# Gated attention with a ternary feed-forward block: decay factors turned by DMA as 16-bit halves instead of by TensorE, and a new order of the work

## The chip, the cores and the metric

The kernel runs on one core of a Trainium2 chip. The metric is the device time of one execution in microseconds; the median of several executions is compared.

## The reference

For x of shape 8 x 1024 x 256 the block adds three terms. What this case touches is `Gc`, one decay factor per token and head, which multiplies the state sum on its way out.

```python
def _L0_attn_ref(x, Wq, Wk, Wv, Wo, gw, sw):        # H = 16 heads of d = 16
    Q, K, V = ((x @ W.T).reshape(B, L, H, d) for W in (Wq, Wk, Wv))
    KV = jnp.einsum('blhd,blhe->blhde', K, V)
    g = jnp.clip(jax.nn.sigmoid(x.reshape(B, L, H, d) @ gw.T), 1e-06, None)
    log_c = jnp.clip(jnp.cumsum(jnp.log(g), axis=1), -30.0, 30.0)
    Gc = (jnp.exp(log_c) + 1e-06)[..., None]
    R = jax.nn.silu(K @ sw.T)[..., None]
    S = jnp.cumsum(KV * R / Gc, axis=1) * Gc
    return jnp.einsum('blhd,blhde->blhe', Q, S).reshape(B, L, D) @ Wo.T

def _L0_ffn_ref(x, fast_b, w_fc, w_proj, u, v, gate):  # hidden 1024, rank 16
    h = _bitlinear(x, w_fc) + gate * (x @ v.T @ fast_b.T @ u.T)
    r = jnp.maximum(h, 0.0)
    return _bitlinear(r * r, w_proj)

xn = _layernorm(x)
return x + _L0_attn_ref(xn, ...) + _L0_ffn_ref(xn, ...)
```

## The kernel before

The tokens are cut into 32 units (b, u) of 256 tokens, each of two chunks c of 128: eight batches, four units each. All engines are programmed by hand, each with its own instruction stream: a `prologue` for the first units, a `slot` that is repeated for the units n = 3 to 29, and an `epilogue`. Within a stream the order is written out, one call per step; a step begins with its waits on semaphores and nothing behind it on that engine can pass it. `slot(b, u)` names its steps by the unit they work on: `prev`, (b, u), `nxt`, `after`, or `unit_after(b, u, k)` for the k-th unit ahead.

The steps for one unit are these. VectorE and ScalarE normalise the tokens (`stats_of`, `rstd_guess`, `refine_rstd`), GpSimd writes them (`normalise`, `xt_low`) and SyncE turns them with a transposing DMA (`turn_tokens`, two 16-bit parts, 1024 columns). TensorE makes queries (`queries_t`, bank front_b), keys (`keys`, bank front_a), values and gates (`values_gates`, front_b) and the cumulated logarithms (`cumulate`, front_a). ScalarE and VectorE take them out of the banks in a high and a low 16-bit part (`queries_high`, `queries_low` and so on), and SyncE spreads them over the lanes with DMAs (`stack_queries` eight, `stack_keys` four). Then per chunk: four `scores` products groups, each masked by VectorE (`mask`), `values` (32 column-tiled products), `state_update` and `carried` on TensorE, `carry_state` and `chunk_out` on VectorE. The feed-forward part is four quarters of `hidden` (ten products), `rectified`, `squares` and `squares_high` on ScalarE, `squares_low` on VectorE and `projected` (eight products). `attn_projected` adds the attention part to bank y, `scale_y` and `residual` (GpSimd) finish, and SyncE stores.

The decay factors take this way. `clip_log` on VectorE writes log_c from front_a. `decay_exp` (line 960) on ScalarE writes exp(-log_c) to `decay`, 32 numbers per token row. `repeat_decay` (line 630) on GpSimd repeats each 16 times into `decay_rep`. `decay_rows` (line 2109) on TensorE turns the four 128x128 blocks into front_a, `decay_transposed` (line 972) on ScalarE copies them to `decay_t`, and `chunk_out` (line 1679) multiplies by them. `keys` of the next unit writes the same bank, so it waits for `decay_t_done`. In the slot `decay_rows(*nxt)` is the last step of TensorE and `decay_transposed(*nxt)` the last of ScalarE.

Steps that are named later: `squares_low` line 1692, `mask` line 1645, `projected` line 2215, `scores` line 2125, `carried` line 2173, `cumulate` lines 2096 and 2097, `queries_t` line 2046, `diagonal_state` line 645, the weight comparisons of GpSimd's prologue `fc_lows` (line 719) and `proj_lows` (line 726), and the clears of v_pad there (line 704).

## Time and profile before

| | us |
|---|---|
| median of three runs | 673.9 |
| lowest, highest | 671.57, 674.31 |
| the profiled execution, its own time | 672.07 |
| its span, first to last instruction | 670.2 |
| TensorE busy in the span | 647.2 |
| VectorE, ScalarE, GpSimd busy | 489.0, 419.1, 339.6 |

Times of steps are from the profiled execution, and positions are microseconds from the start of its span. A busy time is the time in which an engine had an instruction under way; matmuls overlap, so a step's cost on TensorE is read from the spacing of the starts, which the chain of waits does. PE is TensorE, DVE VectorE, ACT ScalarE, POOL GpSimd, SPq the queue of SyncE that issues DMAs. "x32" behind a piece is its number of instructions.

### The profile page before, as it was taken

How to read it: one execution, taken by the hardware profiler on the slowest of the kernel's cores; microseconds unless marked ns; L12 is line 12 of the kernel's file. 1: busy time of each engine (PE TensorE's matmuls, PEld its weight loads, DVE VectorE, ACT ScalarE, POOL GpSimd, SP SyncE). 2: the span in 40 equal slices, each digit the busy share in tenths (PEclk: the TensorE clock that was granted, in tenths of full speed). 3: DMA queues.
4: the chain of work that ended last, by engine and by line, in shares of the span. 5: the costliest groups of instructions: out<-in, count | busy, mean ns of one | idle time of the engine just before them, and what ended most of it. 6: DMA issues, size and time to landing. Idle time of an engine off the chain costs nothing.

```text
span 670.2 us, 21517 instructions
## 1 busy us (share of the span) xinstructions
PE 647.2 (97%) x7862; PEld 564.2 (84%) x7862; DVE 489.0 (73%) x1245; ACT 419.1 (63%) x999; POOL 339.6 (51%) x434
## 2 busy tenths in 40 slices
PE   3879999999999999999999999999999999999997
PEld 3668888888888888888888888888888888888886
DVE  4798986777777677777777777776777776767564
ACT  2577656667756656775566677566567755666771
POOL 4775585344555444455544445554444555443344
PEclk9999999999999999999999999999999999999999
DMA  9244374354444435554554645554454444435220
GB/s 317 71 104 109 75 148 118 104 128 119 99 106 123 111 101 131 115 108 108 113 107 110 125 104 116 108 119 99 117 131 109 106 112 113 102 100 116 68 53 33
DMA packets 153001, 74.66 MB, mean 111 GB/s; under 512 B 84528, under 2 KB 152368, under 8 KB 152896
## 3 DMA queue, kind: packets, MB, share of 16 engines
q1 hardware_dynamic: 150656, 70.66, 45.4%
q10 hardware_dynamic: 2240, 2.62, 1.1%
q8 instruction: 63, 1.03, 0.7%
q14 instruction: 42, 0.34, 0.2%
HBM read 12.43 MB, written 8.39 MB: 31 GB/s over the span
## 4 chain that ended last, share of the span: by engine, by line
PE 90%; POOL 4%; DMA 2%; issue 1%; DVE 1%; SPq 1%; ACT 1%; POOLq 0%; DVEq 0%; ACTq 0%
PE y_bank L2215 16%; PE attn_bank L2159 8%; PE hid_b L2194 8%; PE hid_a L2194 8%; PE front_b L2084 7%; PE y_bank L2229 7%; PE front_a L2065 6%; PE front_b L2046 6%; PE attn_bank L2173 4%; PE score_a L2125 4%; PE score_b L2125 4%; PE attn_bank L2144 3%; PE hid_a L2196 2%; PE hid_b L2196 2%; PE front_a L2109 2%; DMA x_sb<-in_x 2%
## 5 line engine op out<-in xcount | busy, mean ns | idle before, releaser
L645 POOL TENSOR_TENSOR state_diag<-state,state_mask 128x256 f32<-128x256 f32 x56 | 41.3, 738 | 186.1 <-DVE state L1664 142.1
L2215 PE MATMUL y_bank<-wproj_t,sq_h 128*128 128x256 f16 x512 | 117.1, 273 | 0.0
L2215 PE MATMUL y_bank<-wproj_t,sq_l 128*128 128x256 f16 x512 | 117.0, 273 | 0.0
L1645 DVE TENSOR_TENSOR masked<-score_a,shapes_sb 128x512 f32<-128x512 f32 x128 | 87.7, 686 | 26.6 <-PE score_a L2125 26.5
L1692 DVE TENSOR_TENSOR sq_l<-relu_sq,sq_h 128x512 f16<-128x512 f32 x128 | 99.6, 780 | 2.5 <-ACT sq_h L999 2.0
L1645 DVE TENSOR_TENSOR masked<-score_b,shapes_sb 128x512 f32<-128x512 f32 x128 | 87.5, 683 | 18.1 <-PE score_b L2125 18.1
L1008 ACT ACTIVATE relu_sq<-relu_sq 128x512 f32<-128x512 f32 x128 | 81.5, 636 | 3.3 <-DVE sq_l L1692 0.6
L999 ACT ACTIVATE sq_h<-relu_sq 128x512 f16<-128x512 f32 x128 | 80.4, 629 | 1.0 <-PE y_bank L2215 0.9
L630 POOL TENSOR_TENSOR decay_rep<-decay,ones 128x512 f32<-128x512 f32 x32 | 34.5, 1078 | 81.2 <-ACT decay L960 81.2
L2194 PE MATMUL hid_b<-xt,wfc_t 128*128 128x256 f16 x512 | 73.3, 273 | 0.0
L2194 PE MATMUL hid_a<-xt,wfc_t 128*128 128x256 f16 x512 | 73.3, 273 | 0.0
L2159 PE MATMUL attn_bank<-masked,v_pad 128*32 128x128 f32 x2048 | 67.8, 273 | 0.1
L988 ACT ACTIVATE relu_sq<-hid_b,hid_scale 128x256 f32<-128x256 f32 x128 | 53.8, 477 | 15.9 <-PE hid_b L2196 15.8
L2084 PE MATMUL front_b<-wvg_h,xt 128*128 128x304 f16 x256 | 60.6, 295 | 0.9 <-DVE q L1556 0.8
L854 ACT ACTIVATE xn<-xn 128x512 f16<-128x512 f32 x32 | 20.2, 631 | 63.7 <-POOL xn L594 63.7
L988 ACT ACTIVATE relu_sq<-hid_a,hid_scale 128x256 f32<-128x256 f32 x128 | 53.5, 471 | 7.9 <-PE hid_a L2196 7.9
L2215 PEld LDWEIGHTS y_bank<-wproj_t,sq_h 128*128 128x128 f16 x512 | 52.5, 103 | 6.3 <-issue 1.4
L2159 PEld LDWEIGHTS attn_bank<-masked,v_pad 128*32 128x32 f32 x2048 | 53.6, 110 | 1.8 <-issue 1.5
L2194 PEld LDWEIGHTS hid_a<-xt,wfc_t 128*128 128x128 f16 x512 | 50.0, 98 | 6.0 <-DMA z_stack<-z 0.2
L2194 PEld LDWEIGHTS hid_b<-xt,wfc_t 128*128 128x128 f16 x512 | 50.1, 98 | 5.8
L2215 PEld LDWEIGHTS y_bank<-wproj_t,sq_l 128*128 128x128 f16 x512 | 50.1, 98 | 5.4
L2046 PE MATMUL front_b<-xt,wqk 128*128 128x256 f16 x384 | 48.4, 277 | 2.2 <-DVE wqk L1341 1.6
(191 smaller groups left out, 1578.3 us busy)
## 6 DMA issues: line engine op xcount, KB each, us to landing
q_diag<-q SPq DMA_DIRECT2D x256, 64.0 KB, 2.7
k_stack<-k SPq DMA_DIRECT2D x128, 128.0 KB, 3.7
x_sb<-in_x SPq DMA_DIRECT2D x32, 256.0 KB, 3.0
out_y<-y_both SPq DMA_DIRECT2D x32, 256.0 KB, 2.4
relu_sq<-in_w_fc ACTq DMA_DIRECT2D x1, 1024.0 KB, 10.7
pj_nat<-in_w_proj ACTq DMA_DIRECT2D x1, 1024.0 KB, 13.4
y_both<-in_w_qk ACTq DMA_DIRECT2D x1, 512.0 KB, 4.4
w_stage<-in_w_qkvz_t SPq DMA_DIRECT2D x1, 512.0 KB, 6.3
```

The source lines that it names most:

```text
L988: last = nc.scalar.activation(relu[:, n, half], hid_bank[n][:, half], ACT.Relu, scale=hid_scale[:, 2 * q + i:2 * q + i + 1])
L999: nc.scalar.activation(sq_h[:, q], relu[:, q % 2], ACT.Square).then_inc(sq_h_done, 1)
L1008: nc.scalar.activation(sq[:, n], relu[:, n], ACT.Square).then_inc(sq_done, 1)
L1645: nc.vector.tensor_tensor(masked[:, c, g].rearrange("p (h n) -> p h n", h=4), score_bank[g % 2][:].rearrange("p (h n) -> p h n", h=4), cau ...
L1692: nc.vector.tensor_tensor(sq_l[:, q], sq[:, n], sq_h[:, q], ALU.subtract).then_inc(sq_l_done, 1)
L2046: last = mm(front_b[:, o * UNIT:(o + 1) * UNIT], wqk[:, w, t, o * P:o * P + P], xs[:, at, :, t], start=(o == n == 0), stop=(n == 3 * KT - ...
L2084: last = mm(front_b[:, 0:VG], part[:, at, c, t], w[:, t], start=(n == 0), stop=(n == 3 * KT - 1), skip_group_check=True)
L2125: last = mm(score_bank[g % 2][:, i * 2 * P:(i + 1) * 2 * P], k_stack[:, par, g, c, i], q_diag[:, par, 2 * g + i, :, c * P:(c + 1) * P], st ...
L2159: last = mm(attn_bank[32 * q:32 * q + 32, half * P:half * P + P], v_pad[:, par, c, 8 * half + 2 * q + odd], masked[:, c, pair // 2, at:at ...
L2194: mm(place, wfc_t[:, t, j * P:j * P + P], part[:, at, :, t], start=(t == 0 and part is xt_h), stop=False)
L2215: last = mm(y_bank[:, c * D:(c + 1) * D], part[:, q, at:at + P], wproj_t[:, 2 * q + i], start=(q == i == c == n == 0), stop=False, skip_gr ...
L2229: last = mm(y_bank[:, c * D:(c + 1) * D], lhs[:, par, c, t], rhs[:, t], start=False, stop=True, skip_group_check=True)
```

## The change

The turn of the decay factors leaves TensorE. `split_decay` on GpSimd views the 32-bit factors as pairs of 16-bit words and writes all lower halves, then all upper halves, each repeated 16 times: 2 x 2 x 256 words per row, in place of `repeat_decay`. `turn_decays` on SyncE turns these eight 128x128 blocks of 16-bit words with one transposing DMA into the new tile `turned_halves`. `decay_transposed` on ScalarE then writes each half to its place in `decay_t`, 1024 words where it copied 512 numbers before. `decay_rows` is gone, and `keys` waits only for `clip_log` to have read front_a.

```diff
 F32R = mybir.dt.float32r
 F16 = mybir.dt.float16
 I32 = mybir.dt.int32
+U16 = mybir.dt.uint16
 ALU = mybir.AluOpType
 ACT = mybir.ActivationFunctionType
 AX = mybir.AxisListType
...
         write_full = sb("write_full", [P, CH, H])
         write_rec = sb("write_rec", [P, CH, H])
         write = sb("write", [P, 2, CH, H])
-        decay_rep = sb("decay_rep", [P, CH, D])
+        decay_halves = sb("decay_halves", [P, 2, CH, D], U16)
+        turned_halves = sb("turned_halves", [P, 2, CH, KT, P], U16)
         decay_t = sb("decay_t", [P, 2, CH, KT, P])
         v_pad = sb("v_pad", [P, 2, CH, H, 2 * HD])
         masked = sb("masked", [P, CH, 4, 512])
...
         rank_nat = decay_t[:].rearrange("p u c t n -> p (u c t n)").rearrange("p (t n) -> p t n", t=HT)
         w_lane = q_t[:].rearrange("p u t n -> p (u t n)").rearrange("p (w t n) -> p w t n", w=2, t=KT)
-        reach = decay_rep[:].rearrange("p c d -> p (c d)")[:, 0:HT * RANK].rearrange("p (t k) -> p t k", t=HT)
+        reach = decay_halves[:].rearrange("p s c d -> p (s c d)").bitcast(F32)[:, 0:HT * RANK].rearrange("p (t k) -> p t k", t=HT)
         front_a = psum("front_a")
         front_b = psum("front_b")
...
         k_full = sem("k_full")
         vg_full = sem("vg_full")
         cum_full = sem("cum_full")
-        decay_full = sem("decay_full")
+        decay_turned = [sem("decay_turned_even"), sem("decay_turned_odd")]
         xt_h_done = sem("xt_h_done")
         xt_l_done = sem("xt_l_done")
         vg_done = sem("vg_done")
...
         decay_done = sem("decay_done")
         write_step = sem("write_step")
         write_done = sem("write_done")
-        decay_rep_done = sem("decay_rep_done")
+        decay_split_done = sem("decay_split_done")
         decay_t_done = sem("decay_t_done")
         v_pad_done = sem("v_pad_done")
         score_full = sem("score_full")
...
                 sp.dma_start(z_stack[:, u], z16[:, u % 2].rearrange("p c n -> p (c n)"),
                              transpose=True).then_inc(z_turned[u % 2], 16)
+            def turn_decays(b, u):
+
+                if not exists(b):
+                    return
+                sp.wait_ge(decay_split_done, upto(b, u, 1, 0))
+                pb, pu = unit_after(b, u, -1)
+                if exists(pb):
+
+                    sp.wait_ge(decay_t_done, upto(pb, pu, 1, 0))
+                sp.dma_start(turned_halves[:].rearrange("p s c t n -> p (s c t) n"),
+                             decay_halves[:].rearrange("p s c d -> p (s c d)"),
+                             transpose=True).then_inc(decay_turned[u % 2], 16)
+
             def turn_keys(b, u):
                 if not exists(b):
...
                     pool.wait_ge(v_cleared, 2)
                 nc.gpsimd.tensor_tensor(v_heads(par, c, 0, H), val, fac, ALU.mult).then_inc(v_pad_done, 1)
-            def repeat_decay(b, u):
+            def split_decay(b, u):
                 if not exists(b):
                     return
...
                 pb, pu = unit_after(b, u, -1)
                 if exists(pb):
-                    pool.wait_ge(decay_full, upto(pb, pu, 1, 0))
-                nc.gpsimd.tensor_tensor(decay_rep[:].rearrange("p c (h e) -> p (c h) e", e=HD),
-                                        heads_bc(decay[:].rearrange("p c h -> p (c h)"), HD),
-                                        ones[:, 0:HD].unsqueeze(1).to_broadcast([P, CH * H, HD]),
-                                        ALU.mult).then_inc(decay_rep_done, 1)
+                    pool.wait_ge(decay_turned[pu % 2], turned_upto(pb, pu))
+                halves = decay[:].rearrange("p c h -> p (c h)").bitcast(U16).rearrange("p (x s) -> p s x", s=2)
+                nc.gpsimd.tensor_copy(decay_halves[:].rearrange("p s c (h e) -> p s (c h) e", e=HD),
+                                      heads_bc(halves, HD)).then_inc(decay_split_done, 1)
             def diagonal_state(b, u, c):
...
                 pb, pu = unit_after(b, u, -1)
                 if exists(pb):
-                    act.wait_ge(decay_rep_done, upto(pb, pu, 1, 0))
+                    act.wait_ge(decay_split_done, upto(pb, pu, 1, 0))
                     act.wait_ge(write_step, upto(pb, pu, 2, 0))
                 nc.scalar.activation(decay[:], log_c[:], ACT.Exp, scale=-1.0).then_inc(decay_done, 1)
             def decay_transposed(b, u):
                 if not exists(b):
                     return
-                act.wait_ge(decay_full, upto(b, u, 1, 0))
+                act.wait_ge(decay_turned[u % 2], turned_upto(b, u))
                 pb, pu = unit_after(b, u, -2)
                 if exists(pb):
                     act.wait_ge(attn_done, upto(pb, pu, CH, CH - 1))
                 if first_of_all(b, u):
                     act.wait_ge(rank_filled, 2)
-                nc.scalar.activation(decay_t[:, u % 2], front_a[:].rearrange("p (c t n) -> p c t n", c=CH, t=KT),
+                words = decay_t[:, u % 2].rearrange("p c t n -> p (c t n)").bitcast(U16).rearrange("p (x s) -> p s x", s=2)
+                nc.scalar.activation(words, turned_halves[:].rearrange("p s c t n -> p s (c t n)"),
                                      ACT.Copy).then_inc(decay_t_done, 1)
             def rectified(b, u, q):
...
                     pe.wait_ge(wqk_l_done, 2)
                 pb, pu = unit_after(b, u, -1)
                 if exists(pb):
-                    pe.wait_ge(decay_t_done, upto(pb, pu, 1, 0))
+                    pe.wait_ge(log_c_done, upto(pb, pu, 1, 0))
                 at = nth(b, u) % TBUFS
                 for c in range(CH):
                     n = 0
...
                 mm(cum, causal_sb, log_den[:].rearrange("p c h -> p (c h)"), start=True, stop=False)
                 mm(cum, ones[:], before[:, u % 2].rearrange("p c h -> p (c h)"), start=False,
                    stop=True).then_inc(cum_full, 1)
-
-            def decay_rows(b, u):
-
-                if not exists(b):
-                    return
-                pe.wait_ge(log_c_done, upto(b, u, 1, 0))
-                pe.wait_ge(decay_rep_done, upto(b, u, 1, 0))
-                for c in range(CH):
-                    for t in range(KT):
-                        at = (c * KT + t) * P
-                        last = nc.tensor.transpose(front_a[:, at:at + P], decay_rep[:, c, t * P:t * P + P], ident_sb)
-                last.then_inc(decay_full, 1)
             def scores(b, u, c, g):
```

The order of every stream is new. The five slots after the change (SyncE, GpSimd, ScalarE, VectorE, TensorE):

```diff
             def slot(b, u):
                 nxt, prev, after = unit_after(b, u, 1), unit_after(b, u, -1), unit_after(b, u, 2)
+                stack_queries(*after)
+                turn_keys(*after)
                 turn_tokens(*unit_after(b, u, 3))
+                load(*unit_after(b, u, 5))
                 store(*prev)
+                stack_keys(*after)
+                turn_z(*after)
+                turn_decays(*after)
...
             def slot(b, u):
                 nxt, prev, after = unit_after(b, u, 1), unit_after(b, u, -1), unit_after(b, u, 2)
+                attn_high(b, u, 0)
+                weigh_values(*nxt, 1)
+                residual(*prev)
                 xt_low(*unit_after(b, u, 3))
+                attn_low(b, u, 0)
+                split_decay(*after)
+                diagonal_state(*nxt, 0)
+                normalise(*unit_after(b, u, 4), 0)
                 attn_high(b, u, 1)
                 attn_low(b, u, 1)
+                normalise(*unit_after(b, u, 4), 1)
+                weigh_values(*after, 0)
+                diagonal_state(*nxt, 1)
...
             def slot(b, u):
                 nxt, prev, after = unit_after(b, u, 1), unit_after(b, u, -1), unit_after(b, u, 2)
+                decay_exp(*after)
+                squares_high(*nxt, 0)
+                rstd_guess(*unit_after(b, u, 4))
+                squares(b, u, 3)
+                squares(*nxt, 0)
+                rectified(*nxt, 1)
+                queries_high(*unit_after(b, u, 3))
+                queries_full(*unit_after(b, u, 3))
+                squares(*nxt, 1)
+                squares_high(*nxt, 1)
+                rectified(*nxt, 2)
+                xt_high(*unit_after(b, u, 4))
+                squares_high(*nxt, 2)
+                values_gates(*unit_after(b, u, 3), 0)
+                keys(*unit_after(b, u, 3))
+                keys_high(*unit_after(b, u, 3))
+                values_gates(*unit_after(b, u, 3), 1)
+                squares(*nxt, 2)
+                gate_exp(*unit_after(b, u, 3))
+                z_high(*unit_after(b, u, 3))
+                rectified(*nxt, 3)
+                gate_log(*unit_after(b, u, 3))
+                decay_transposed(*after)
+                squares_high(*nxt, 3)
+                rectified(*after, 0)
...
             def slot(b, u):
                 nxt, prev, after = unit_after(b, u, 1), unit_after(b, u, -1), unit_after(b, u, 2)
+                scalars_of(*unit_after(b, u, 4))
+                carry_state(*nxt, 0)
+                clip_log(*after)
+                chunk_out(*nxt, 0)
+                mask(*nxt, 1, 2)
+                squares_low(b, u, 2)
+                mask(*nxt, 1, 3)
+                squares_low(b, u, 3)
+                refine_rstd(*unit_after(b, u, 4))
+                write_factors(*after)
+                stats_of(*unit_after(b, u, 5))
+                queries_low(*unit_after(b, u, 3))
+                squares_low(*nxt, 0)
+                mask(*after, 0, 0)
+                mask(*after, 0, 1)
+                carry_state(*nxt, 1)
+                mask(*after, 0, 2)
+                mask(*after, 0, 3)
+                chunk_out(*nxt, 1)
+                scale_y(b, u)
+                keys_low(*unit_after(b, u, 3))
+                waits_for_stats(*unit_after(b, u, 5))
+                moments_of(*unit_after(b, u, 5))
+                mask(*after, 1, 0)
+                dens(*unit_after(b, u, 3))
+                z_low(*unit_after(b, u, 3))
+                mask(*after, 1, 1)
+                sums_before(*unit_after(b, u, 3))
+                squares_low(*nxt, 1)
...
             def slot(b, u):
                 nxt, prev, after = unit_after(b, u, 1), unit_after(b, u, -1), unit_after(b, u, 2)
+                projected(b, u, 1)
+                queries_t(*unit_after(b, u, 3))
+                projected(b, u, 2)
+                state_update(*nxt, 1)
+                values(*nxt, 1)
+                carried(*nxt, 1)
+                hidden(*nxt, 2)
+                scores(*after, 0, 0)
+                scores(*after, 0, 1)
+                projected(b, u, 3)
+                keys(*unit_after(b, u, 3))
+                scores(*after, 0, 2)
+                values_gates(*unit_after(b, u, 3), 0)
+                scores(*after, 0, 3)
+                attn_projected(b, u)
+                scores(*after, 1, 0)
+                values_gates(*unit_after(b, u, 3), 1)
+                hidden(*nxt, 3)
+                scores(*after, 1, 1)
+                state_update(*after, 0)
+                values(*after, 0)
+                scores(*after, 1, 2)
+                projected(*nxt, 0)
+                hidden(*after, 0)
+                carried(*after, 0)
+                cumulate(*unit_after(b, u, 3))
+                scores(*after, 1, 3)
+                hidden(*after, 1)
```

The slot's range, units 3 to 29, is the same, but the slot now works one unit further ahead: the scores in it are those of unit u+2, the queries of u+3, the projection quarters 1 to 3 of u and quarter 0 of u+1. The prologues are longer by about a unit and the epilogues shorter. In GpSimd's prologue `repeat_decay(0, 0)` stood between `proj_lows(0)` and `proj_lows(1)`; now `clear_values(1)` stands there and `split_decay(0, 0)` comes after both and after the tokens of unit (0, 2). In VectorE's prologue `columns_low(0)` and `refine_rstd(0, 1)` come ahead of `group_scales()`, and in ScalarE's `rstd_guess(0, 1)` ahead of `fc_sums(0)`.

## Rows read from the trace of the kernel before

**Rows 1.** the page's part 1: engine, busy us, share of the span, instructions

```profile
PE 647.2 (97%) x7862; PEld 564.2 (84%) x7862; DVE 489.0 (73%) x1245; ACT 419.1 (63%) x999; POOL 339.6 (51%) x434
```

**Rows 2.** busy time by stretches: PE, PEld, DVE, ACT, POOL, granted clock, DMA, GB/s

```profile
0.00:50.00 50.00, 32.26 (x195) 26.20 (x196) 36.53 (x122) 25.67 (x69) 32.26 (x36) 1.00 0.56 163
50.00:100.00 50.00, 49.78 (x660) 43.19 (x659) 43.58 (x103) 32.55 (x76) 32.74 (x40) 1.00 0.52 111
...
300.00:350.00 50.00, 50.00 (x615) 44.08 (x614) 35.85 (x95) 29.67 (x72) 25.85 (x34) 1.00 0.55 107
```

**Rows 3.** the chain of waits, one unit's middle: start us, us, what

```profile
308.01 1.31 PE front_b L2046 x12
...
318.65 0.87 PE attn_bank L2159 x32
319.52 0.64 PE attn_bank L2173 x4
...
323.15 0.34 PE front_a L2096 x2
...
324.58 0.45 PE attn_bank L2173 x4
325.03 0.87 PE y_bank L2215 x8
...
327.34 0.44 PE front_a L2109 x4
327.78 1.31 PE front_b L2046 x12
```

**Rows 4.** waits of TensorE after 50 us: us in total, times, longest

```profile
PE score_a L2125 <- issue: 0.4, 1, 0.4
PE score_a L2125 <- DVE masked L1645: 0.2, 1, 0.2
```

**Rows 5.** the chain of waits in the first 80 us

```profile
35.78 1.48 issue
...
37.30 1.36 POOL decay_rep L630
...
57.90 0.33 PE score_a L2125 x2
...
69.47 0.14 PE front_a L2096 x2
```

**Rows 6.** groups of GpSimd instructions: busy us, mean ns, idle before

```profile
L630 POOL TENSOR_TENSOR decay_rep<-decay,ones 128x512 f32<-128x512 f32 x32 | 34.5, 1078 | 81.2 <-ACT decay L960 81.2
...
L726 POOL TENSOR_SCALAR y_both<-pj_nat,pj_scale 128x1024 f16<-128x1024 f32 x2 | 5.8, 2923 | 0.0
...
L704 POOL MEMSET v_pad<- 128x1024 f32 x2 | 1.9, 952 | 0.0
...
L713 POOL COPY state_mask<-state_mask 128x128 f32<-128x128 f32 x1 | 0.3, 291 | 0.0
```

**Rows 7.** groups of ScalarE instructions

```profile
L972 ACT ACTIVATE decay_t<-front_a 128x512 f32<-128x512 f32 x32 | 19.1, 598 | 25.7 <-PE front_a L2109 25.7
...
L1073 ACT ACTIVATE sq_h<-pj_nat 128x1024 f16<-128x1024 f32 x2 | 2.1, 1054 | 0.0
```

**Rows 8.** DMA issues: count, KB, median us from issue to landing

```profile
k_stack<-k SPq DMA_DIRECT2D x128, 128.0 KB, 3.7
...
xt<-xn SPq DMA_TRANSPOSE x32, 3.1
```

**Rows 9.** timeline, all engines: start us, us, engine, line

```profile
312.23 5.16 SPq L454 DMA_DIRECT2D q_diag<-q  x8
...
312.41 0.69 DVE L1645 TENSOR_TENSOR masked<-score_a,shapes_sb 128x512 f32<-128x512 f32 x1 [0.24 <-PE score_a L2125]
...
313.64 0.73 POOL L645 TENSOR_TENSOR state_diag<-state,state_mask 128x256 f32<-128x256 f32 x1
...
313.77 1.15 DVE L1692 TENSOR_TENSOR sq_l<-relu_sq,sq_h 128x512 f16<-128x512 f32 x1
```

840 lines of the change are left out of this document (387 added, 453 removed).

## Prediction

> **What bounds the kernel now.** The page's engine table comes first: TensorE is busy for 647.2 of 670.2 us [rows 1], more than any other engine. A share of busy time is only a hint, so the next view is the busy time by stretches. Between 300 and 350 us TensorE is busy for the whole 50.00 us at full granted clock while VectorE has 35.85, ScalarE 29.67 and GpSimd 25.85; the first 50 us are different, with TensorE busy for 32.26 [rows 2]. The waits of TensorE after 50 us confirm it: two, together 0.6 us [rows 4]. So from 50 us to the last unit every instruction of TensorE is time of the kernel, and nothing else is. The chain of waits in the middle of the run then gives the price of each step, since it holds nothing but TensorE there. It is read as the spacing of the work, not as the duration of one instruction, because matmuls overlap. The query products of two successive units start at 308.01 and 327.78, 19.77 us apart [rows 3].
>
> **Part 1, the four turning products go.** They stand on that chain in each unit: 0.44 us for four [rows 3], one unit after the other, 32 units. 32 x 0.44 = 14.1 us; by the finer spacing of 0.109 us (eight products of y take 0.87 us [rows 3]) 128 x 0.109 = 14.0 us. I take 14.0. Nothing fills the hole by waiting, if parts 2 to 4 hold.
>
> **Part 2, the new order on TensorE.** No product is added. What the order can change is the cost of a change of shape. After the 32 column-tiled products of `values` the next step is dearer than elsewhere. `carried` takes 0.64 us after `values` and 0.45 after a projection; the first half of `cumulate` takes 0.34 after `values` and 0.14 elsewhere; a score pair takes 0.33 after `values` [rows 3, 5] against two spacings of 0.109, 0.22. Before, a unit has `values` then `carried` (+0.19) and `values` then `cumulate` (+0.20). After, it has `values` then `carried` (+0.19) and `values` then `scores` (+0.11). That is 0.09 us less in each of the 27 units of the loop, less in a few where `carried` or the state update is left out: 0.09 x 24 = 2.2 us. The bounds are 0 and 5 us on this side; the same size, 5 us, is possible the other way if a neighbour pair that the old trace doesn't have (`carried` after `hidden`, `cumulate` after `carried`) is dear.
>
> **Part 3, the added steps, off TensorE.**
> - GpSimd: `split_decay` writes 1024 16-bit elements per partition where `repeat_decay` wrote 512 of 32 bits in 1.08 us. A plain copy of 128 elements takes 0.29 us, a comparison of 1024 takes 2.92 [rows 6]. By bytes it costs 1.06, by elements at the copy's rate (0.29 less a start of some 0.1, over 128, is 1.5 ns each) 1.6 us, and 2.9 is the far end. I take 1.6: it is a copy, and nearest to the copy's row. GpSimd has half its time free [rows 2], so this costs nothing by itself.
> - SyncE: `turn_decays` is one more transposing DMA of 1024 16-bit columns, the very size of the token transpose, which lands 3.1 us after its issue [rows 8]. On its queue it stands last in the slot, behind `stack_keys` and `turn_z`, and waits for `split_decay`. Queued behind it is only the next `stack_queries`, eight issues of 5.16 us together [rows 9], whose input, by the walk through the slot (part 4), comes some 5 us later.
> - ScalarE: `decay_transposed` handles 1024 elements, not 512. The 512 take 0.60 us, a plain activation over 1024 takes 1.05 [rows 7], so +0.45 us a unit on an engine with 20 of 50 us free [rows 2]. The bounds are 0 and 0.5 us more, should a 4-byte output step be dear.
> - The path is log_c, exp, split (1.6), DMA (3.1), ScalarE (1.05). The new slot lays it over a whole unit: log_c of unit u+2 comes at the end of one slot, `decay_transposed` for it is almost last in ScalarE's next slot, about 15 us later, and its reader `chunk_out` is in the slot after. The path needs about 7 us. Slack is some 8 us, so the cost is 0. A wait also vanishes: `keys` on TensorE waited for `decay_t` of the unit before (bank front_a was lent to the turn) and now waits for log_c only.
>
> The Trainium skill speaks against the swap: "VectorE: DVE Perf Modes", section The three transpose paths, gives 1309 ns for a 128x128 16-bit tile by DMA against 390 ns by TensorE. By that figure eight tiles one after the other would be an estimated 10.5 us in place of 3.1 us and would eat nearly all the slack; by the token transpose's row, the same eight tiles, they don't. Either way the sum stays the same unless the slack is overrun.
>
> **Part 4, the order on the other engines, tightest links.** TensorE's new slot of about 19.2 us was walked through with the prices of rows 3. Three links are tight.
> - `carried(u+1,1)` must end before ScalarE may copy the full queries; then VectorE does `queries_low`, `squares_low`, the first mask, and `scores(u+2,0,2)` waits for that mask. TensorE has between them `hidden` (ten products, 1.09), two score pairs 0.44, `projected` 0.87 and `keys` 1.31 = 3.7 us. The other side is 0.60 for ScalarE [rows 7] and three VectorE operations of about 0.69 [rows 9] = 2.7 us. Slack 1.0 us.
> - `projected(u,2)` waits for `squares_low(u,2)`. In the walk VectorE reaches it about 2.1 us ahead of the deadline and needs 0.69; what can delay it is the first rival.
> - The tokens: `scale_y`, `residual`, `xt_low`, the transpose (3.1 us [rows 8]), `queries_t`. Slack about 2.4 us.
> So the cost is 0, and what would be late first is the second link.
>
> **Part 5, start and end.** In the first 50 us TensorE stands idle for 17.7 us [rows 2]. The chain there runs through GpSimd's weight comparisons, and `repeat_decay(0,0)` sits in the middle of them: 1.48 us of waiting for its input and 1.36 us itself [rows 5]. The new prologue puts `split_decay(0,0)` behind both projection comparisons and takes one clear of v_pad ahead (0.95 us [rows 6]): 2.8 - 0.95 = 1.9 us. VectorE also finishes rstd of unit (0,1) before the group scalings, so GpSimd starts its chain some 1 to 2.4 us earlier. Lower bound 0 (another engine takes over as limit; VectorE is the candidate), upper 4.3; I take 3.0. The end keeps its steps and order almost as they are: 0, within 1 us.
>
> **The sum.** 14.0 + 2.2 + 3.0 = 19.2 us. Span 670.2 - 19.2 = 651.0 us. The profiled execution took 672.07 us, 1.9 us beyond its span: 652.9. The median of the runs shown, 673.9, lies 1.8 above the profiled one: 654.7 us.
>
> **The rivals.**
> A. The port that VectorE and GpSimd share. The trace shows it: a 128x512 `squares_low` (two SBUF inputs) that begins at 313.77 during a GpSimd operation of 313.64 to 314.37 takes 1.15 us, and 0.60 us of it lie behind the other's end [rows 9]. In the new slot `split_decay` begins at about the time when VectorE reaches `squares_low(u,2)`. With a copy of 1.6 us VectorE is held for some 1.0 us and 0.4 us of slack are left; from a copy of about 2.1 us on, TensorE waits. With the 2.9 us end and `diagonal_state` (0.73) taking the port directly behind it, the step is late by about 1.5 us in each of 28 units: 42 us, 654.7 + 42 = 697 us, slower than before. With the copy alone at 2.9, 0.8 x 28 = 22 us, 677 us, 0.4% above the old median. The Trainium skill ("SBUF — State Buffer", section Who interferes with whom) says the same, that whichever of the two starts first holds the pair for its whole instruction; here the trace agrees with 1.15 us, and the price hangs on the copy's length alone. Against it: the half-free GpSimd, and a copy's row of 0.29 us for 128 elements. Chance 5% for the slow end, 3% for the middle.
> B. Only the turning products count: start and order give nothing. 673.9 - 14.0 = 659.9 us. For it: from 50 to 100 us VectorE is busy for 43.58 of 50 us [rows 2], so an earlier start may only meet VectorE. Chance 22%.
> C. Small waits: the new order leaves 0.1 to 0.4 us of TensorE idle in each unit where the old had none, for example at the mask link when the keys or tokens land late behind the extra transpose (k_stack lands 3.7 us after issue [rows 8]). 28 x 0.25 = 7 us: 654.7 + 7 = 662, with 668 at the far end. Chance 12%.
> D. The change doesn't do what it says: the turn comes back as a wait on SyncE's one queue, with `decay_transposed` waiting and behind it `rectified`, which feeds `hidden`. It decides once the DMA path needs over 15 us; at the slack of 8 us and a landing of 3.1 this wants it three to four times as long. It would give back the 14 us and more: about 675 us. Chance 3%.
>
> **How the numbers follow.** My forecast, TensorE without a wait, 655 us within 5, has 55%; B 22%, C 12%, A 8%, D 3%. Predicted time 654.7 us. Low end 649.5: order at 5 and start at 4.3 would be 650.6, a run 1 us lower. High end 665: it takes in B and the larger part of C. Outside are A, D and the far end of C, some 13%, and a few per cent below. A change under 0.5% (3.4 us) can't be told from none here. Faster by more than that: the forecast, B and C, 0.89; within 0.5%: the middle of A and D, 0.06; slower: the slow end of A, 0.05.
>
> **What would show each step right or wrong.** No product of front_a from the decay tile; query products of successive units 19.2 to 19.4 us apart; TensorE busy for all of 300 to 350 us and its waits after 50 us below 2 us. The split copy between 1.1 and 2.1 us; `decay_t` written in about 1.05 us with no VectorE wait on it; the transpose landing in 3 to 4 us. TensorE idle in the first 50 us near 15 us. Wrong would be: a wait of TensorE for `sq_l` (rival A), for a mask or for k_stack (C), or ScalarE's wait for the turned halves followed by TensorE's for relu (D).

## The result, and the profile after

The changed kernel takes 653.3 us (median of four runs, 652.8 to 654.9) against 672.7 for the kernel before: ratio 0.9714, interval 0.9683 to 0.9745. It is 19.4 us faster. The profiled execution took 652.8 us with a span of 651.0; the prediction had 654.7, 652.9 and 651.0.

The page's part 1 of the changed kernel, columns as in [rows 1]:

```profile
PE 629.2 (97%) x7734; PEld 546.5 (84%) x7734; DVE 507.5 (78%) x1245; ACT 435.3 (67%) x999; POOL 357.1 (55%) x434
```

Its busy time by stretches, columns as in [rows 2]:

```profile
0.00:50.00 50.00, 33.31 (x230) 28.06 (x230) 41.03 (x129) 28.95 (x77) 31.67 (x38) 1.00 0.59 173
50.00:100.00 50.00, 50.00 (x662) 43.31 (x661) 41.59 (x100) 35.63 (x82) 30.07 (x36) 1.00 0.69 124
300.00:350.00 50.00, 50.00 (x615) 43.60 (x613) 39.73 (x98) 34.71 (x81) 25.64 (x31) 1.00 0.55 123
```

Against [rows 1] TensorE lost 18.0 us of busy time, VectorE gained 18.5, ScalarE 16.2 and GpSimd 17.5, and the kernel became faster all the same: only TensorE's stretch is full. Which part of the change cost them that, the turn or the order, is read below from the variant with the new order and the turn on TensorE. After 50 us TensorE waited once, where [rows 4] have two waits:

```profile
PE score_a L2161 <- issue: 0.4, 1, 0.4
```

The chain of waits in the middle, where [rows 3] stood (start us, us, what; L2094 are the queries, L2195 `values`, L2209 `carried`, L2161 `scores`, L2251 `projected`, L2144 the first half of `cumulate`):

```profile
307.51 0.87 PE attn_bank L2195 x32
308.38 0.32 PE score_a L2161 x2
308.71 0.87 PE y_bank L2251 x8
...
310.67 0.45 PE attn_bank L2209 x4
311.12 0.14 PE front_a L2144 x2
...
313.67 1.31 PE front_b L2094 x12
314.98 0.87 PE y_bank L2251 x8
...
316.21 0.87 PE attn_bank L2195 x32
317.09 0.64 PE attn_bank L2209 x4
...
332.93 1.31 PE front_b L2094 x12
```

There is no piece for the turn. The queries stand 19.26 us apart (313.67 to 332.93), where [rows 3] had 19.77. The neighbour prices are as read before: scores after `values` 0.32, `carried` after `values` 0.64. The two pairs that the old trace didn't have are no dearer than elsewhere: `carried` after `hidden` 0.45, `cumulate` after `carried` 0.14.

The new steps, in the groups of instructions (busy us, mean ns, idle before):

```profile
L1727 DVE TENSOR_TENSOR sq_l<-relu_sq,sq_h 128x512 f16<-128x512 f32 x128 | 105.3, 824 | 1.0 <-ACT relu_sq L1032 0.9
...
L666 POOL TENSOR_TENSOR state_diag<-state,state_mask 128x256 f32<-128x256 f32 x56 | 53.4, 954 | 63.6 <-DVE state L1699 63.1 <-DVE state L1694 0.4
...
L996 ACT ACTIVATE decay_t<-turned_halves 128x1024 uint16<-128x1024 uint16 x32 | 43.0, 1345 | 0.5 <-DMA turned_halves<-decay_halves 0.5
...
L653 POOL COPY decay_halves<-decay 128x1024 uint16<-128x1024 uint16 x32 | 33.2, 1038 | 87.3 <-ACT decay L983 87.3
```

The view of the tile `turned_halves`:

```profile
DMA to landing us min/median/max: 3.0/3.2/5.4
```

The split copy takes 1.04 us, no more than the multiplication that it replaces [rows 6]. The join takes 1.34 where the copy from the bank took 0.60 [rows 7], and waits for its DMA once in 32 times, for 0.5 us. The shared port shows at the place that rival A named (timeline, start us, us):

```profile
312.04 1.04 POOL L653 COPY decay_halves<-decay 128x1024 uint16<-128x1024 uint16 x1 [3.30 <-ACT decay L983]
...
312.57 1.05 DVE L1727 TENSOR_TENSOR sq_l<-relu_sq,sq_h 128x512 f16<-128x512 f32 x1
...
313.04 1.18 POOL L666 TENSOR_TENSOR state_diag<-state,state_mask 128x256 f32<-128x256 f32 x1
```

`squares_low` starts half a microsecond before the copy ends and takes 1.05 us in place of 0.67. It is done at 313.62, and its reader `projected` starts in the same timeline at 314.82: 1.2 us of slack. (The chain of waits above has 314.98 for that start: its stamps lie 0.16 us behind the timeline's here, so the two aren't mixed.)

### The profile page after: what moved, and what is told of

The parts are those of the page before. It is cut to its first block, busy times and chain, and to the rows that moved or that the text cites. A ratio compares the mean times of both kernels' runs of the same rounds, so it can differ in the third digit from the quotient of the medians.

```text
span 651.0 us, 21292 instructions
## 1 busy us (share of the span) xinstructions
PE 629.2 (97%) x7734; PEld 546.5 (84%) x7734; DVE 507.5 (78%) x1245; ACT 435.3 (67%) x999; POOL 357.1 (55%) x434
## 4 chain that ended last, share of the span: by engine, by line
PE 92%; DMA 3%; SPq 2%; DVE 1%; issue 1%; POOL 0%; POOLq 0%; DVEq 0%
PE y_bank L2251 17%; PE attn_bank L2195 9%; PE hid_b L2230 9%; PE hid_a L2230 9%; PE front_b L2132 7%; PE y_bank L2265 7%; PE front_a L2113 6%; PE front_b L2094 6%; PE score_a L2161 5%; PE attn_bank L2209 5%; PE score_b L2161 4%; PE attn_bank L2180 3%; PE hid_a L2232 2%; PE hid_b L2232 2%; DMA x_sb<-in_x 2%
## 5 line engine op out<-in xcount | busy, mean ns | idle before, releaser
L2251 PE MATMUL y_bank<-wproj_t,sq_h 128*128 128x256 f16 x512 | 118.5, 273 | 0.0
L2251 PE MATMUL y_bank<-wproj_t,sq_l 128*128 128x256 f16 x512 | 118.5, 273 | 0.0
L1727 DVE TENSOR_TENSOR sq_l<-relu_sq,sq_h 128x512 f16<-128x512 f32 x128 | 105.3, 824 | 1.0 <-ACT relu_sq L1032 0.9
L666 POOL TENSOR_TENSOR state_diag<-state,state_mask 128x256 f32<-128x256 f32 x56 | 53.4, 954 | 63.6 <-DVE state L1699 63.1
L1032 ACT ACTIVATE relu_sq<-relu_sq 128x512 f32<-128x512 f32 x128 | 79.6, 623 | 9.8 <-DVE sq_l L1727 9.7
L653 POOL COPY decay_halves<-decay 128x1024 uint16<-128x1024 uint16 x32 | 33.2, 1038 | 87.3 <-ACT decay L983 87.3
L697 POOL TENSOR_TENSOR y_both<-y_both,x_sb 128x512 f32<-128x512 f32 x32 | 41.2, 1287 | 70.0 <-DVE y_both L1739 70.0
L933 ACT ACTIVATE vg<-front_b 128x304 f32<-128x304 f32 x64 | 27.2, 425 | 71.9 <-PE front_b L2132 71.8
L2195 PE MATMUL attn_bank<-masked,v_pad 128*32 128x128 f32 x2048 | 67.8, 273 | 0.0
L1012 ACT ACTIVATE relu_sq<-hid_a,hid_scale 128x256 f32<-128x256 f32 x128 | 53.4, 470 | 17.5 <-PE hid_a L2232 17.1
L898 ACT ACTIVATE q_t<-front_b 128x512 f32<-128x512 f32 x32 | 19.1, 597 | 61.1 <-PE attn_bank L2209 61.1
L616 POOL TENSOR_SCALAR xn<-x_sb,neg_mean,rstd 128x256 f32<-128x256 f32 x64 | 35.8, 561 | 43.9 <-DVE rstd L1583 43.9
L1591 DVE TENSOR_TENSOR q<-front_b,q 128x512 f16<-128x512 f32 x32 | 22.1, 691 | 46.6 <-ACT q_t L898 46.5
L2251 PEld LDWEIGHTS y_bank<-wproj_t,sq_h 128*128 128x128 f16 x512 | 50.1, 98 | 6.1 <-DVE sq_l L1727 0.3
```

Of the source, the lines that this page charges most:

```text
L666: nc.gpsimd.tensor_tensor(state_diag[:].rearrange("p t (g s e) -> p (t g) s e", s=2, e=HD), lanes.unsqueeze(2).to_broadcast([P, KT * 4, 2, ...
L1012: last = nc.scalar.activation(relu[:, n, half], hid_bank[n][:, half], ACT.Relu, scale=hid_scale[:, 2 * q + i:2 * q + i + 1])
L1032: nc.scalar.activation(sq[:, n], relu[:, n], ACT.Square).then_inc(sq_done, 1)
L1727: nc.vector.tensor_tensor(sq_l[:, q], sq[:, n], sq_h[:, q], ALU.subtract).then_inc(sq_l_done, 1)
L2195: last = mm(attn_bank[32 * q:32 * q + 32, half * P:half * P + P], v_pad[:, par, c, 8 * half + 2 * q + odd], masked[:, c, pair // 2, at:at ...
L2251: last = mm(y_bank[:, c * D:(c + 1) * D], part[:, q, at:at + P], wproj_t[:, 2 * q + i], start=(q == i == c == n == 0), stop=False, skip_gr ...
```

## The experiments

Times are medians, ratios are to the kernel before on the same chip. The changed kernel itself, run again, is the base for small differences. The spare products, the early join, `refine_rstd` and `projected` were run in a session of their own, where the kernel before took 673.8 us against 673.0 beside the base; so differences of theirs under 1 us mean nothing. Units are counted from 1, and a unit's place is the start of its queries.

> The changed kernel once more, beside the three others of this job, so that they can be compared on one chip. Expected 653.3 us within 1; span 651 us.

Measured: 652.79 us (652.37 to 653.06), ratio 0.9694 (0.9673 to 0.9715), span 651.0.

### What the four products cost

One variant puts four turning products of a constant tile ahead of each unit's keys:

```diff
                 at = nth(b, u) % TBUFS
+                for j in range(CH * KT):
+                    nc.tensor.transpose(front_a[:, j * P:j * P + P], ident_sb, ident_sb)
```

> The changed kernel with four extra turning products of a constant tile ahead of the keys of each unit, into the bank that the keys then overwrite; nothing waits for them and their result isn't used. Theory (each product is time of TensorE and nothing hides it): 32 units x 0.44 = 14.0 us more, 666.8 us. Rival (the old turn cost more than its products, by its waits in the loop): the same here, but the difference to the kernel before, 6.2 us, would then have to be found in waits of the old loop; it had 0.6 us, so the rest is order and start.

Measured: 667.55 us, ratio 0.9911 (0.9895 to 0.9927), 14.8 above the base, span 15.0 above. The chain shows the products and the unit, 19.70 us:

```profile
301.71 1.31 PE front_b L2094 x12
...
308.17 0.44 PE front_a L2110 x4
...
321.41 1.31 PE front_b L2094 x12
```

The term of 14.0 us holds. Of the span's 15.0, 10.3 lie between the ninth and the last unit's queries (23 groups of 0.44 are 10.1), 4.2 before them, where eight groups are 3.5, and 0.4 behind. So most of the excess lies in the start, which differs from run to run (the third unit's queries began at 48.5, 49.0 and 49.6 us in profiles of kernels with one and the same prologue), and in this profile the granted clock there stood at the lower level, 1.2 GHz, for 3.4 us from 36.7 on.

The other variant takes the whole turn of the kernel before (repeat, TensorE's products, copy from the bank) into the new order, with `decay_rows(u+2)` behind `carried(u+1, 1)` and the copy behind the full queries:

```diff
                 carried(*nxt, 1)
+                decay_rows(*after)
                 hidden(*nxt, 2)
```

> The new order, with the turn back on TensorE behind carried(u+1,1), the repeat on GpSimd and the 512-element copy on ScalarE. Theory: the loop's unit is 0.44 us longer than with the DMA turn, 14 us in all; the order alone keeps its 1.4 us in the loop and about 3 us at the start. Time 653.3 + 14.0 = 667 to 669 us, 3.5 to 5.5 below before. Rival (the order gives nothing by itself): 672.7 us.

Measured: 685.3 us, ratio 1.0174 (1.0155 to 1.0194): slower than the kernel before, a miss of 17 us. The loop did as expected, 19.69 us a unit without a wait. The loss is in the first 150 us, by stretches:

```profile
0.00:50.00 50.00, 31.60 (x176) 25.55 (x177) 34.75 (x111) 23.54 (x62) 30.37 (x36) 0.90 0.56 161
50.00:100.00 50.00, 44.26 (x538) 37.44 (x539) 34.26 (x91) 30.99 (x78) 21.98 (x27) 0.97 0.41 78
100.00:150.00 50.00, 46.78 (x598) 39.52 (x587) 36.64 (x89) 27.85 (x66) 24.25 (x31) 0.97 0.45 111
```

and in TensorE's waits after 50 us:

```profile
PE front_a L2137 <- POOL decay_rep L632: 5.8, 3, 2.7
```

In the prologue the turn stood directly ahead of the next unit's keys, and TensorE waited there for `decay_rep`, and the keys for `decay_t` (3.1 us more). The granted clock fell with the waits: 0.90, 0.97 and 0.97 in the three stretches of 50 us, where the changed kernel has 1.00. That is an estimated 8 us of full-speed work at most. At the seventh unit's queries this kernel was 21.6 us behind the changed one (143.35 against 121.76); products, waits and clock together are about that. So the total says something of that placement, and only the loop says something of the products.

Together they split the gain of the loop. Four units (one batch) take 78.31 us before (queries from 151.22 to 229.53), 78.10 with the new order and four products a unit (203.76 to 281.86; the same 78.1 with the real turn), and 76.34 after (198.66 to 275.00). The products are 1.76 of 1.97 us a batch, the order 0.21.

The same run tells whose the added busy time is. Its page's part 1:

```profile
PE 651.8 (95%) x7862; PEld 565.0 (83%) x7862; DVE 507.1 (74%) x1245; ACT 412.9 (60%) x999; POOL 357.0 (52%) x434
```

VectorE and GpSimd are as busy here as with the DMA turn (507.5 and 357.1), so their 18 and 17 us come from the new order and not from the turn: `diagonal_state`, for one, averages 0.95 us in both and 0.74 in the kernel before. Only ScalarE's time changes with the turn, by 22.4 us (412.9 to 435.3), and the new order itself had saved it 6.2.

### Whether the DMA turn needs the new order

The old order, with the DMA turn between `stack_keys` and `turn_z` on SyncE and the join last in ScalarE's slot, where the copy from the bank was:

```diff
                 stack_keys(*nxt)
+                turn_decays(*nxt)
                 turn_z(*nxt)
```

> The order of before, with only the turn changed: split on GpSimd, one transposing DMA on SyncE between stack_keys and turn_z, the join on ScalarE at the end of the slot. Theory (the DMA path nearly fits the old slot): 14.0 us of TensorE go in all; in a full slot ScalarE ends the join about 0.9 us later than the old copy, under the 1.2 us that the low queries had to spare, so no loss in the loop; at the start ScalarE waits about 3 to 4 us for the first turned halves. Time 672.7 - 14.0 + 4 = 663 us. Rival (the path needs the new order): TensorE waits in each unit for something behind the join, 0.4 us or more, and the time is 670 us or more.

Measured: 694.5 us, ratio 1.0317 (1.0279 to 1.0356), 31 us above the expectation; its rival had "670 us or more". Undisturbed units take 19.34 us (307.12 to 326.46), 0.43 less than before, as the theory says; but the first 150 us and several later units are worse. Stretches of it:

```profile
0.00:50.00 50.00, 26.61 (x146) 21.40 (x146) 33.43 (x112) 18.31 (x51) 30.12 (x34) 0.93 0.60 167
50.00:100.00 50.00, 44.39 (x561) 37.52 (x561) 38.34 (x88) 35.20 (x80) 25.61 (x31) 0.94 0.48 93
...
300.00:350.00 50.00, 50.00 (x628) 43.88 (x626) 36.04 (x98) 31.26 (x74) 27.39 (x36) 1.00 0.60 129
```

ScalarE's wait over the whole run:

```profile
ACT decay_t L993 <- DMA turned_halves<-decay_halves: 88.8, 31, 11.1
```

ScalarE waits for the halves in 31 of 32 units, 2.9 us each, where the new order waits once. From the eighth unit's queries to the last unit's, this kernel took 468.3 us and the one before 470.0: 24 units gave 1.7 us, not 10.5, the other 8.8 went in single late units. At the eighth unit's queries it was already 17.6 us behind; the granted clock was 0.93, 0.94 and 0.93 there, behind TensorE's waits. In the late units TensorE waited not for the join but for the keys: each of these waits of the products of `scores`, up to 1.3 us, ends 0.09 us after the last `k_stack` transfer of the unit landed. The longest wait, at the end, is for z, whose transfer stands in SyncE's queue behind the decay turn, which stood there for its split copy:

```profile
662.27 1.25 SPq L495 DMA_TRANSPOSE turned_halves<-decay_halves  x1
663.62 1.20 SPq L483 DMA_TRANSPOSE z_stack<-z  x1
```
```profile
PE hid_a L2203 <- DMA z_stack<-z: 6.7, 1, 6.7
```

So here the DMA turn in the old order loses more than it saves; how much of the start's loss is due to the prologue written for this test was not tried.

In the new order, the join right behind `decay_exp` in ScalarE's slot takes the slack away:

```diff
                 decay_exp(*after)
+                decay_transposed(*after)
```

> ScalarE's decay_transposed(u+2) goes right behind decay_exp(u+2), so that the DMA path has no slack and ScalarE itself stands still for it. Path behind exp: split copy 1.0 (and what GpSimd does ahead of it), issue and landing 3.2, queue ahead of it on SyncE. Theory (the place of the join is what makes the DMA turn free): ScalarE waits some 7 us a unit; it is busy for 35 of 50 us in the loop, so 19.3 us a unit has 5.8 us to spare and the unit becomes at least 20.5 us: above 685 us, likely about 700. Rival (ScalarE's slack swallows it): 652.8 to 655 us.

Measured: 788.6 us, ratio 1.1709 (1.1684 to 1.1733). ScalarE's waits after 100 us:

```profile
ACT decay_t L996 <- DMA turned_halves<-decay_halves: 184.4, 27, 8.6
ACT vg L933 <- PE front_b L2132: 46.8, 54, 1.9
ACT relu_sq L1012 <- PE hid_a L2232: 43.3, 27, 2.2
```

TensorE's waits after 50 us:

```profile
PE y_bank L2251 <- DVE sq_l L1727: 83.1, 27, 4.4
PE score_a L2161 <- DVE masked L1680: 12.2, 9, 1.4
```

The decay path of one unit in the timeline:

```profile
316.55 1.04 POOL L653 COPY decay_halves<-decay 128x1024 uint16<-128x1024 uint16 x1 [2.99 <-ACT decay L983]
...
320.24 2.13 SPq L495 DMA_TRANSPOSE turned_halves<-decay_halves  x1
...
323.83 1.34 ACT L996 ACTIVATE decay_t<-turned_halves 128x1024 uint16<-128x1024 uint16 x1 [7.34 <-DMA turned_halves<-decay_halves]
```

The wait is 184.4 / 27 = 6.8 us a unit, as expected, and the path can be read off: 1.04 for the copy, 2.65 until SyncE's queue comes to it, 3.6 to the landing. But the unit became 24.2 us (queries of 24 units from 148.86 to 728.63), not 20.5. ScalarE's free 5.8 us didn't soak the wait up, since that free time is itself waiting for TensorE (0.9 us twice and 1.6 us once a unit in the waits above), and TensorE in turn now waits 3.1 us for `squares_low`, which hangs on the squares behind the join. The granted clock fell too, to 0.94 over these 24 units, but that is at most half a us of the unit. Six units at the full clock, with queries from 271.21 to 413.08, took 23.6 us each:

```profile
271.20:413.10 141.90, 116.31 (x1427) 98.50 (x1425) 89.55 (x221) 78.02 (x180) 63.44 (x77) 1.00 0.48 104
```

Waits of engines that feed each other added up here; they didn't overlap as free time does in a table.

### The port that VectorE and GpSimd share

Two variants add the same extra elements ahead of the split copy, three copies of 1024 halves or one of 3072:

```diff
+                nc.gpsimd.tensor_copy(spare_halves0[:].rearrange("p s c (h e) -> p s (c h) e", e=3 * HD),
+                                      heads_bc(halves, 3 * HD))
                 nc.gpsimd.tensor_copy(decay_halves[:]...
```

> GpSimd makes three more split copies of 1.04 us each, into spare tiles, ahead of the real one: 4.15 us in place of 1.04. Theory of the shared port (it is held for one instruction): VectorE gets in between two copies and squares_low is not later than now; what is late is diagonal_state and with it carried(u+1,1), by 0 to 0.5 us a unit. Time 653 to 668 us, and TensorE's wait, if any, is for state_diag. Rival (the port doesn't matter, GpSimd's total does): the same time as with one long copy of the same total.

> The same extra work as with three short copies, but as one instruction of 3072 elements per partition, about 3.1 us. Theory of the shared port: squares_low(u,2) is held until the long copy ends, is 0.8 us late for projected(u,2), and 28 x 0.8 = 22 us come on top: 675 us, with a squares_low of over 3 us in the trace and TensorE waiting for sq_l. Rival (no hold by one instruction): the time of three short copies within 2 us, and squares_low as long as there.

Measured: 679.2 us with three short (ratio 1.0091, 1.0062 to 1.0120), 677.7 with one long (1.0064, 1.0048 to 1.0080). Three short copies cost more than the 653 to 668 us expected, one long copy was expected at 675. The totals lie within 2 us of each other, which is what the rival (only GpSimd's total matters) had said of them; what differs is the traces, and they alone speak for the port. Three short copies, groups of instructions:

```profile
L1738 DVE TENSOR_TENSOR sq_l<-relu_sq,sq_h 128x512 f16<-128x512 f32 x128 | 112.6, 881 | 1.0 <-ACT relu_sq L1043 0.9
...
L660 POOL COPY spare_halves<-decay 128x1024 uint16<-128x1024 uint16 x32 | 47.7, 1490 | 0.0
```

TensorE's longest wait there:

```profile
PE attn_bank L2220 <- POOL state_diag L677: 22.3, 27, 2.4
```

One long copy, groups of instructions:

```profile
L1732 DVE TENSOR_TENSOR sq_l<-relu_sq,sq_h 128x512 f16<-128x512 f32 x128 | 165.1, 1291 | 1.0 <-ACT relu_sq L1037 0.9
...
L656 POOL COPY spare_halves<-decay 128x3072 uint16<-128x3072 uint16 x32 | 87.8, 2742 | 87.3 <-ACT decay L988 87.3
```

TensorE's longest wait, and then one piece of the chain of waits:

```profile
PE y_bank L2256 <- DVE sq_l L1732: 13.2, 27, 1.7
```
```profile
325.88 2.76 DVE sq_l L1732
```

Behind the long copy a single `squares_low` lasts 2.76 us and TensorE waits for it in 27 units, which is rival A's mechanism at its far end, a copy of 2.7 us. The loop's unit is 0.64 us longer on average (a batch 78.92 us in place of 76.34). With short copies `squares_low` averages 0.88 and gets in between; then GpSimd's own queue is late, since the second and third copy, held in their turn, take 1.49 and 1.44 us, and `carried` waits for `state_diag`: 0.83 us a unit (a batch 79.65 us). So how long VectorE is held hangs on the length of the one instruction that holds the port; the kernel's time doesn't hang on that alone, since a GpSimd queue that is late costs as much.

### Where the start's gain comes from

Two moves of the prologue, each undone by itself: `split_decay(0, 0)` back between the two projection comparisons on GpSimd (first diff), and `refine_rstd(0, 1)` back behind `group_scales` on VectorE (second).

```diff
                 proj_lows(0)
-                clear_values(1)
+                split_decay(0, 0)
                 proj_lows(1)
```
```diff
-                refine_rstd(0, 1)
                 group_scales()
+                refine_rstd(0, 1)
```

> In GpSimd's prologue split_decay(0, 0) and clear_values(1) change places, so that the split stands between the two projection comparisons as the repeat did before. Theory (GpSimd's chain bounds the start): the split waits for its input some 2 us, the second comparison ends 2 to 3 us later, and 1 to 2.5 us show at the end: 655 us. Rival (the start is bound by the way of the first keys to their stack): no change, 653.3 us, the first score products still at 40.3 us of the span.

> Only the start: on VectorE refine_rstd(0, 1) goes back behind group_scales, where the kernel before had it. Theory (part of the gain at the start is that GpSimd's normalise(0, 1) and all behind it on its queue begin earlier): 1 to 2.5 us more, 653.8 to 655.3. Rival (the start was bounded by something else, such as the keys' DMAs): 652.8, no change.

Measured: 656.4 us for the first (ratio 0.9749, 0.9727 to 0.9771), 3.6 above the base, and TensorE waits for the projection weights inside the first 50 us. Behind that wait the granted clock stood at 1.2 GHz for 3.4 us (from 44.7), so a part of the 3.6 is likely the clock's:

```profile
PE y_bank L2068 <- DVE pj_nat L1506: 2.6, 1, 2.6
```

The second: 654.4 us (ratio 0.9727, 0.9704 to 0.9749), 1.6 above the base. That isn't clear of noise, since the base's interval (0.9673 to 0.9715) overlaps. Three executions with a mean granted clock of 1.00 took 653.7 to 654.4 us; the two at 0.995, of which one is the profile, took 656.5 and 657.0, and in the profile the clock stood at 1.2 GHz for 6.8 us from 36.6 on. For the first move the rival of an unmoved start falls: GpSimd's chain through the comparisons set it. For the second it is likely and not shown.

### Three other places in TensorE's slot

Scores of unit u+2 directly behind `values`; `carried(u+2, 0)` directly behind `values`; and `projected(u, 2)` between `values` and `carried`:

```diff
                 values(*nxt, 1)
+                scores(*after, 0, 0)
                 carried(*nxt, 1)
                 hidden(*nxt, 2)
-                scores(*after, 0, 0)
```
```diff
                 values(*after, 0)
+                carried(*after, 0)
                 scores(*after, 1, 2)
                 projected(*nxt, 0)
                 hidden(*after, 0)
-                carried(*after, 0)
```

```diff
-                projected(b, u, 2)
                 state_update(*nxt, 1)
                 values(*nxt, 1)
+                projected(b, u, 2)
                 carried(*nxt, 1)
```

> In TensorE's slot scores(u+2,0,0) goes ahead of carried(u+1,1), so that a score pair (0.33 us there, 0.22 elsewhere) and not carried (0.64, 0.45 elsewhere) follows the column-tiled values. Theory of the neighbour costs: 0.08 us less in each of 27 units, and the 0.22 us by which carried is later fits the slack of the mask link: 653.3 - 2.2 = 651.1 us, loop period per batch of four units 76.35 - 0.32 = 76.0 us. Rival (the extra goes with carried, not with its neighbour): no change.

> The counter test: carried(u+2,0) moves to stand right behind values(u+2,0), ahead of the score pair. Theory of the neighbour costs: 0.08 us more in each of 24 units: 653.3 + 1.9 = 655.2 us, period per batch 76.35 + 0.24 to 0.32 us, unless carried there also waits for the masked state. Rival: no change.

> In TensorE's slot projected(b, u, 2) moves from ahead of state_update(u+1, 1) to between values(u+1, 1) and carried(u+1, 1). Theory (a product that follows the column-tiled products of values is dearer, by 0.19 us for carried and 0.10 for the y products): carried loses its 0.19, projected gains 0.10, so 0.09 us less in each of 27 units, 2.4 us: 650.4 us, with no new wait (the link from the second mask to values has 1.9 us of slack and loses 0.87; squares_low to projected(u,2) gains slack). Rival (the price belongs to the change itself and moves whole to whatever follows): 652.8 us, no change. Second rival (a link was tighter than read, as it was with scores first): above 654, with a wait of TensorE for attn masks or issue.

Measured: 663.5, 655.7 and 651.3 us; ratios 0.9846 (0.9818 to 0.9874), 0.9743 (0.9718 to 0.9769), 0.9673 (0.9656 to 0.9691). With `carried` behind `values` the unit is 19.35 us instead of 19.26 and the batch 0.28 longer, as priced; of the 2.9 us in all 1.7 lie in the loop's 24 units. Scores first, expected at 651.1 us, was a miss of 12 us. It made the bare unit shorter (19.17), but TensorE waited for it:

```profile
PE score_a L2161 <- issue: 10.6, 13, 2.0
```

The scores came `carried` and `hidden` earlier, 0.64 + 1.09 = 1.7 us, and the expectation had looked at `carried`'s slack only, not at theirs. The trace names no releaser ("issue"), but its landings do: all 13 waits end 0.09 us after the last of the unit's four `k_stack` transfers landed, while the queries' had landed some 8 to 11 us before. In the changed kernel that landing lies 0.1 to 2.9 us ahead of its reader, 1.6 in the median, so 1.7 us was more than half the units had. With `projected` between, the unit is 19.17 us, and after 50 us TensorE waits twice, 0.9 us for the keys' transfer and 0.2 for a mask:

```profile
315.12 0.87 PE attn_bank L2195 x32
315.99 0.98 PE y_bank L2251 x8
316.97 0.45 PE attn_bank L2209 x4
```

`projected` pays 0.11 and `carried` saves 0.19. That is 2.2 us over 27 units in the spacing. Of it the profiled execution kept 0.2 (span 650.8): its third unit began 1.1 us later and the unit with the wait for the keys stretched by 1.1. The medians differ by 1.5 us, but the intervals of the two ratios overlap: the unit is shorter, the kernel perhaps, by less than these runs resolve.

## Why the prediction held, step by step

- **TensorE bounds the loop, so its products are time of the kernel.** Right. 14.0 us predicted; 14.8 us when four were put back, 0.44 a unit in the chain.
- **The sum.** 19.2 us forecast and 19.2 measured in the span, to the tenth, is luck: the order was taken 0.8 too large and the start 0.8 too small. The median came 1.4 below the forecast because it lies 0.5 above the profiled execution and not 1.8.
- **The order.** Right in kind, too large: 2.2 us predicted (0.09 in 24 units), 0.21 a batch, 1.4 us over 27 units, measured. In whole units it is 0.07 to 0.08 (19.77 less 0.44 less 19.26 or 19.25). In one unit of four, though, the order gives nothing: at a batch's first unit one `carried` is left out, and before it was the dear one behind `values` (0.64), now it is the cheap one behind `hidden` (0.45). The step "less in a few" should have been read out.
- **The start.** 3.0 predicted; 19.2 less 14.0 less 1.4 leaves 3.8. Of the two causes named the split's place was shown, with 3.6 us when undone, the clock's part in it included; `refine_rstd`'s place gave 1.6 us, which the runs hardly resolve. Their sum is more than the whole; that each undone move makes the same chain late is argued, not tested (no run undid both). "TensorE idle near 15 us" was wrong by 1.7: it is 16.7. Of the 3.8 us this view shows 1.0 as idle time less; the rest left TensorE's busy time in the start, beyond products and order, and why was not settled.
- **The split copy.** 1.6 us taken, 1.04 measured: the size goes by bytes, the lower bound. The two ends had stood there, and the choice of the nearest row, a small copy with its fixed part guessed, was the error. It lies just under the 1.1 to 2.1 us that were named as a sign. It cost nothing, since it made rival A's link look tighter (0.4 us of slack) than it was (1.2). Copy and slack together are 2.2 us, close to the copy of 2.1 from which on TensorE was to wait.
- **The join.** 1.05 taken, 1.34 measured, inside the bound for a 4-byte output step. ScalarE had the time.
- **The DMA.** 3.1 taken, 3.2 measured, and slack near 8 us held: in the loop the halves landed 6.7 to 9.7 us ahead of the join, and there was one wait of 0.5 us, in the first unit. The figure of the Trainium skill ("VectorE: DVE Perf Modes", section The three transpose paths), 1309 ns for each 16-bit tile, doesn't add up for eight tiles in one DMA: 3.2 us here, not the estimated 10.5. Other transfers beside it: `k_stack` landed in 3.8 where [rows 8] have 3.7, `z_stack` in 3.7 us instead of 2.3, the store in 3.4 instead of 2.4, and of them TensorE waited in the loop only for `k_stack`, once, 0.4 us (the wait named "issue" above ends 0.09 us behind its landing).
- **The tight links.** Three were listed, with slacks of 1.0 to 2.4 us. The one that bit when the order was moved, `k_stack` to the first scores, wasn't among them, though its slack is 1.6 us in the median.
- **The rivals.** A needs a copy of over 2.1 us and showed its wait when it was given 2.7. The time, 677.7 us, is that of its middle case (677) partly by luck: of the 25 us 15.4 lie in the loop's 24 units, at 0.64 a unit where 0.8 was reckoned, and 7.6 before them. B (659.9) falls with the measured 653.3 and the first test of the start. C showed only when an order made the links tighter, 10.6 us with scores first, and it was the keys' transfer that rival C had named. D was shown by taking the slack away: 788.6 us, far more than the 675 it was priced at. Its price counted only TensorE's saving as lost, and not that a wait on ScalarE comes back through VectorE and TensorE to itself.

## What to carry to other kernels

Where one engine is full and the others aren't, moving 14 us off it is a gain though ScalarE pays 22 us for the new turn and the new order costs VectorE 18 and GpSimd 17, if the new path has slack. The slack has to be made by the order: with the DMA turn the old order (with a start written for that test) is 21 us slower than the kernel before and the new one 19 faster. Price a step of an added path by where its reader stands in the slot, and a step that is moved by all that it waits for. Read the order's unusual units (here a batch's first) as well as the usual one. An engine's free share didn't absorb a wait here, since its free time was already waiting for the engines behind it.

## What the runs showed of the hardware

- GpSimd copies 1024 16-bit elements, spread from 64, in 1.04 us, about as long as its 32-bit multiplication of half as many takes (1.08), and 3072 in 2.74.
- ScalarE writes 1024 16-bit elements at a step of 4 bytes in 1.34 us, against 1.05 for 1024 32-bit inputs to packed 16-bit.
- The hold on the port goes both ways: beside `squares_low` on VectorE GpSimd's copies rose from 1.04 to 1.49 us and `diagonal_state` from 0.73 to 1.18. The Trainium skill's rule ("SBUF — State Buffer", section Who interferes with whom), one holds the pair for its whole instruction, agrees with the 2.76 us of `squares_low` behind the 2.74 us copy.
- A change from column-tiled products to others costs TensorE 0.19 to 0.20 us ahead of 32-bit products (`carried`, `cumulate`) and 0.10 to 0.11 ahead of 16-bit ones (`scores`, `projected`).
- In some profiles TensorE's granted clock fell to 1.2 GHz in the start, behind waits: for 6.8 us with `refine_rstd` late (waits of 2.0 and 1.5 us ahead of it), for 3.4 with the split between the comparisons (2.6). In the changed kernel's own profile, with waits of the same size there, it read 1.00 in the first 50 us.
- One transposing DMA of eight 128x128 16-bit tiles landed 3.2 us after its issue began, in the median of 32 (3.0 to 5.4).
